# Retention queries: two products of all heads copied out twice with a row mask, instead of four products with half of their columns zero

## What is computed

```
q = jnp.einsum('bhsd,hde->bhse', xh, wq)          # complex
k = jnp.einsum('bhsd,hde->bhse', xh, wk)
v = jnp.einsum('bhsd,hde->bhse', xh, wv)
scores = jnp.einsum('bhse,bhte->bhst', q, k) * _decay_mask(s)
y = jnp.einsum('bhst,bhte->bhse', scores, v).real
mu = y.mean(-1, keepdims=True)
var = y.var(-1, keepdims=True)
yn = (y - mu) * jax.lax.rsqrt(var + 1e-05)
...
out = ((gate * yn).astype(jnp.complex64) @ w2).real
```

## Time and profile before

| | |
|---|---|
| median of 3 runs | 2453.52 us (2449.77 to 2454.09) |
| the profiled execution | 2452.1 us, span of its instructions 2450.3 us |
| busy over the span | PE 87%, PEld 61%, DVE 65%, ACT 50%, POOL 37% |
| chain that ended last | the page's list of its lines has only lines of the last stage |
| retention stage | about 522.8 us to 812.7 us of the span, 290 us |

### The profile page before, as it was taken

The page is one execution under the profiler, slowest core; times in us unless marked ns, Lnnn a source line. Parts: engine busy times, 40 slices in busy tenths (PEclk is TensorE's granted clock), DMA queues, the critical chain, the costliest instruction groups (busy, mean ns, idle before and its releaser), DMA issues. The chain is left out here.

```text
span 2450.3 us, 41718 instructions
## 1 busy us (share of the span) xinstructions
PE 2134.8 (87%) x14183; PEld 1496.8 (61%) x14183; DVE 1588.2 (65%) x3564; ACT 1230.3 (50%) x2063; POOL 915.0 (37%) x763
## 2 busy tenths in 40 slices
PE   5799999979998599999999997999999995776671
PEld 4567868855555466666666664777777774555450
DVE  4432333346777588888888875676767664666673
ACT  2334464344554367677667675555655562332330
POOL 0000000013443378777778772000000001786772
PEclk9999999989999699999999999999999996678995
DMA  7660010019920100000000000000000001214554
GB/s 262 245 245 18 27 34 11 1 43 419 420 117 2 69 1 1 0 0 0 0 0 0 0 1 20 1 0 0 0 0 0 0 1 45 83 43 122 165 154 154
DMA packets 64688, 165.46 MB, mean 68 GB/s; under 512 B 12310, under 2 KB 43460, under 8 KB 55084
## 3 DMA queue, kind: packets, MB, share of 16 engines
q1 hardware_dynamic: 51564, 148.42, 17.0%
q0 software_dynamic: 7104, 12.71, 1.5%
q10 hardware_dynamic: 5888, 2.62, 0.4%
HBM read 68.81 MB, written 96.86 MB: 68 GB/s over the span
## 5 line engine op out<-in xcount | busy, mean ns | idle before, releaser
L1261 POOL TENSOR_TENSOR c_both<-c_hid 128x512 f32<-128x512 f32 x384 | 491.6, 1287 | 144.5 <-ACT c_hid L1234 106.2
L1234 ACT ACTIVATE c_hid<-c_scaled,c_b 128x1024 f32<-128x1024 f32 x384 | 437.1, 1150 | 172.9 <-DVE c_scaled L1308 158.0
L1308 DVE TENSOR_TENSOR c_scaled<-c_p_h,c_shares 128x1024 f32<-128x1024 f32 x384 | 454.5, 1215 | 80.5 <-PE c_p_h L1177 79.5
L1182 PE MATMUL c_p_o<-c_both,c_w 128*128 128x512 f32 x768 | 390.8, 591 | 0.0
L1175 PE MATMUL c_p_h<-c_x_hi,c_w_hi 128*128 128x512 f32 x384 | 291.9, 760 | 2.6 <-DVE c_w_lo L1331 2.6
L624 POOL TENSOR_TENSOR d_ln_rstd<-d_ln_var,d_ln_power 128x2 f32<-128x2 f32 x48 | 33.4, 696 | 525.3 <-DVE d_ln_var L620 525.3
L240 POOL COPY a_work<-a_vec 128x64 f32<-128x64 f32 x4 | 1.2, 303 | 444.4 <-PE a_p_A L322 256.0
L1182 PEld LDWEIGHTS c_p_o<-c_both,c_w 128*128 128x128 f32 x768 | 144.3, 188 | 36.1 <-issue 2.2
L1176 PE MATMUL c_p_h<-c_x_lo,c_w_hi 128*128 128x512 f32 x384 | 152.6, 397 | 0.0
L1492 PEld LDWEIGHTS d_p_s<-d_kk,d_q_bd 128*128 128x128 f32 x768 | 123.9, 192 | 45.9 <-issue 45.9
L1177 PE MATMUL c_p_h<-c_x_hi,c_w_lo 128*128 128x512 f32 x384 | 151.9, 396 | 0.0
(11 more groups left out here) (331 smaller groups left out, 4658.6 us busy)
## 6 DMA issues: line engine op xcount, KB each, us to landing
slots<-b_blank SPq DMA_DIRECT2D x56, 1040.0 KB, 23.7
band_scratch<-a_work SPq DMA_DIRECT2D x16, 1024.0 KB, 5.7
a_work<-band_scratch SPq DMA_DIRECT2D x16, 1023.5 KB, 7.9
e_wb<-e_weights SPq DMA_DIRECT2D x63, 164.0 KB, 2.5
a_raw<-in_Wc SPq DMA_DIRECT2D x16, 512.0 KB, 3.6
e_xb<-slots SPq DMA_DIRECT2D x63, 130.0 KB, 2.2
e_yb<-e_again SPq DMA_DIRECT2D x12, 512.0 KB, 5.6
a_work<-in_x_tok SPq DMA_DIRECT2D x16, 256.0 KB, 8.2
```

Source lines behind the costliest of these rows:

```text
L1182: nc.tensor.matmul(p_o[s][:, 0:N], w2[:, q, :], both[q % SLOTS][:, :], start=(q == 0), stop=(q == NQ - 1)).then_inc(s_down, 1)
L1234: nc.scalar.activation(hid[q % SLOTS][:, :, :], scaled[q % SLOTS][:, :, :], ACT.Gelu, bias=b1[:, q:q + 1]).then_inc(s_ge, 1)
L1261: nc.gpsimd.tensor_tensor(both[q % SLOTS][:, :], hid[q % SLOTS][:, 0, :], hid[q % SLOTS][:, 1, :], ALU.add).then_inc(s_bo, 1)
L1308: v.tensor_tensor(scaled[q % SLOTS][:, :, :], p_h[q % SLOTS][:, 0:N].unsqueeze(1).to_broadcast([128, 2, N]), shares[s][:, :, :], ALU.mult) ...
```

## The change

Queries now come from two products, i = 0 and 1, one for each part, with all columns of the weight in place. ScalarE copies each of the two out twice, with a per-partition scale `half[:, a]` that is one on the rows of head a of every pair and zero on the others. `tq` has the same contents as before. `half` is a new input of 128 x 2 numbers, loaded with the other constants (CONST counts it). NQ falls from 4 to 2 and NP from 6 to 4, so the projections at the end of a body are the values alone. `score_w` is half as large, isn't cleared any more, and is filled by two copies of 128 columns instead of four of 64.

```diff
-        score_w = sb("score_w", [128, 4, 128])
+        score_w = sb("score_w", [128, 2, 128])
+        half = sb("half", [128, 2])
...
-        NQ = 4
+        NQ = 2
         NP = NQ + 2
...
-                             (wv[:, :, :], w["wv"]), (w1[:, :], w["w1"]), (w2[:, :], w["rw2"]), (gn[:, :], w["gn"])):
+                             (wv[:, :, :], w["wv"]), (w1[:, :], w["w1"]), (w2[:, :], w["rw2"]), (gn[:, :], w["gn"]),
+                             (half[:, :], w["half"])):
...
-        CONST = 16 * 6
+        CONST = 16 * 7
...
                     if i < NQ:
-                        nc.scalar.copy(tq[s][:, :, i, :], p_p[i % 2][:, 0:N].rearrange("p (n s) -> p n s", n=GB))\
-                            .then_inc(s_projc, 1)
+                        for a in range(2):
+                            last = nc.scalar.activation(tq[s][:, :, 2 * a + i, :],
+                                                        p_p[i % 2][:, 0:N].rearrange("p (n s) -> p n s", n=GB),
+                                                        ACT.Identity, scale=half[:, a:a + 1])
+                        last.then_inc(s_projc, 1)
                         continue
...
-            act.wait_ge(s_zero, 5)
+            act.wait_ge(s_zero, 4)
+            act.wait_ge(s_const, CONST)
...
-            v.memset(score_w[:, :, :], 0.0).then_inc(s_zero, 1)
...
-            dve.wait_ge(s_zero, 5)
-            for a in range(2):
-                for r in range(2):
-                    heads = "p (j a d) -> p j a d"
-                    last = v.tensor_copy(score_w[:, 2 * a + r, :].rearrange(heads, a=2, d=RD)[:, :, a, :],
-                                         p_p[r][:, 0:128].rearrange(heads, a=2, d=RD)[:, :, a, :])
+            for r in range(2):
+                last = v.tensor_copy(score_w[:, r, :], p_p[r][:, 0:128])
...
+    side = np.arange(128) // RD % 2
+    d["half"] = f(np.stack([side == 0, side == 1], 1).astype(np.float32))
```

## The result

The changed kernel takes 2443.25 us (median of 6 runs, 2441.13 to 2447.97), the kernel before 2453.31 us in the same series (6 runs, 2449.77 to 2454.09). The ratio is 0.9964 with a 95% interval of 0.9951 to 0.9977: faster by 10 us, 0.4%. The forecast was 2444 us, 0.4% faster.

A forecast was written before the change was run, and what follows sets the result against it. TensorE's order and the loop through VectorE and GpSimd's root both take 15.73 us, the second binding after the change. Steady groups 5.5, body 0 1.5 and start 1.6 sum to 8.6 us: forecast 2444 us, range 2438 to 2450.

The forecast's parts named there:

- The bound: Steady groups: TensorE's order and the VectorE-GpSimd root loop both take 15.73 us; once TensorE is faster, the second binds.
- The walk through VectorE's body: VectorE from yn to the variance, TensorE early: pauses before prod and masks 1 close, new interval 15.27 us.
- The term, 12 x 0.46 = 5.5 us: Twelve steady intervals from yn to yn, each 0.46 us shorter: 5.5 us won (2.4 to 7.0).
- The start: Stage start: projections 0.6 us earlier, two products fewer, values falling into the slow-clock stretch: 1.6 us won (1.1 to 3.1).
- Body 0: First body, no yn, TensorE's order sets the pace: the removed pair counts in full, 1.5 us (1.4 to 1.5).
- The last bodies: Last two bodies, without layer norm statistics; masks 2 wait for scores that keep their distance from masks 0: nothing won.
- The sum: Whole kernel: 5.5 + 1.5 + 1.6 = 8.6 us won (4.9 to 11.6).
- The first yn: Sign in the changed kernel's profile: the first yn should start at about 574.4.
- The activation: ScalarE's four scaled query copies: 0.58 us each instead of 479 ns, 0.4 us more per group.
- the wait at the yn columns: TensorE in steady groups of the changed kernel: it should wait some 0.5 us for yn at the yn columns.
- the third rival: ScalarE's queue becomes the bound: threshold 0.7 us per activation, kernel slower from about 0.9; at 1.0, 2457.6 to 2459.0 us; 4%.
- The price of the pair: TensorE, one pair of query products a group: 1.48 us of its time removed.

The follow-up runs named there:

- short_before: Kernel before with GpSimd's root computed for 4 of 32 columns, the rest a constant 1.0: 2448.41 us beside 2454.37, ratio 0.9976.
- short_after: Changed kernel with GpSimd's root computed for 4 of 32 columns, the rest a constant 1.0: 2424.06 us, ratio to the kernel before 0.9879.
- after_again: The changed kernel run once more, nothing altered: ratio to the kernel before 0.9969.
- plain_copies: Changed kernel with the four query copies unscaled, the mask left out: 2445.89 us, ratio to the kernel before 0.9967.
- extra_product: Changed kernel with the first query product computed twice into the same bank: 2446.69 us, ratio to the kernel before 0.9973.
- double_copies: Changed kernel with each scaled query copy done once more into a spare buffer: 2531.68 us beside 2524.31 for the kernel before, ratio 1.0024.
- extra_two: Changed kernel with both query products computed twice into their banks: 2514.30 us beside 2517.58 for the kernel before, ratio 0.9994.

## Why the prediction was right, and where it was off

**The bound (right).** Before, TensorE's loop; after, VectorE's and GpSimd's. short_before and short_after show both halves. One reading was too simple: TensorE does not work "without a break but for 0.73 us". In the kernel before, the fourth scores at 649.47 take 1.26 us instead of 0.90, because they wait for masks 2. It changes nothing in the forecast, since this wait is there with the root cut as well.

**The walk through VectorE's body (right).** Distances from the start of yn, forecast and measured: masks 1 at 2.95 and 2.94, combine at 3.42 and 3.42, statistics at 4.94 and 4.90, masks 2 at 6.92 and 6.88, the variance complete at 9.73 and 9.70. The term, 12 x 0.46 = 5.5 us, came out as 188.78 - 183.28 = 5.50, but from ten intervals of 15.23 or 15.24 (0.49 less than before) and two of 15.43 and 15.51. These two come in the same groups in after_again, plain_copies and extra_product, and in short_after as 14.59 and 14.52. They belong to this program, and I have no cause for them. So the hit of 5.50 against 5.5 is partly luck: each usual interval gave a little more than forecast, and these two gave less.

**The start (right).** From the stage's first DMA to the first masks it was 545.46 - 522.84 = 22.62 us, and is 544.32 - 523.39 = 20.93: 1.69 for the 1.6 forecast. As supposed, the values fell into the slow stretch and took 3.30 us instead of 1.98 (TensorE's timeline, answers to the earlier trace rows):

```profile
534.85 2.93 PE L785 MATMUL b_p_p<-b_xT,b_score_w 128*128 128x384 f32 x4 [0.58 <-DVE b_score_w L1013]
537.73 3.30 PE L791 MATMUL b_p_p<-b_wv,b_xT 128*96 128x256 f32 x8
```

**Body 0 (under-sized).** I had 1.5 us; from the first masks of group 0 to those of group 1 it was 17.52 us and is 15.52, 2.0 less. The removed pair is 1.48 of it. The rest is where the slow clock fell. In the kernel before it took in the gate product, so the second scores and masks 1 came late (masks 1 start 5.36 us behind masks 0), and the third scores waited for masks 1: 1.61 us instead of 0.90 (first fence). In the changed one the gate product still ran fast and combine was slow, masks 1 came 4.33 us behind masks 0, and the third scores did not wait (second):

```profile
547.78 1.54 PE L795 MATMUL b_p_p<-b_xT,b_w 128*128 128x384 f32 x2
549.25 1.55 PE L755 MATMUL b_p_s<-b_tq,b_xT 32*96 32x384 f32 x8
550.73 0.87 PE L765 MATMUL b_p_y<-b_sm,b_val 96*32 96x96 f32 x32
...
552.10 1.61 PE L755 MATMUL b_p_s<-b_tq,b_xT 32*96 32x384 f32 x8
```

```profile
546.37 0.84 PE L797 MATMUL b_p_p<-b_xT,b_w 128*128 128x384 f32 x2
547.14 1.51 PE L757 MATMUL b_p_s<-b_tq,b_xT 32*96 32x384 f32 x8
548.58 1.51 PE L767 MATMUL b_p_y<-b_sm,b_val 96*32 96x96 f32 x32
...
550.91 0.90 PE L757 MATMUL b_p_s<-b_tq,b_xT 32*96 32x384 f32 x8
```

**The last bodies.** Forecast nothing, measured 0.1 us. The sum, forecast as 8.6 us, is 9.3 us in the stage.

**What was luck.** The median of 2443.25 us lies within 1 us of the forecast of 2444, but executions of one kernel differ by 4 to 7 us, and the other stages took 3.4 us of the profiled execution's gain back. The first yn at 574.36, forecast as 574.4, is a coincidence too: the stage started 0.55 us later and won 0.6 us more on the way there than forecast.

**ScalarE.** The activation took 581 ns for 580. The queue had more room than I gave it: some 0.6 us around the values' copies, and 0.99 us between the loops instead of the 0.5 of the wait at the yn columns. The step that was off is that I took a visible wait for the whole slack. It left the forecast untouched, but it set the third rival's threshold too near.

**The price of the pair.** 1.48 us is right for what the loop lost (short_before and short_after), but putting the pair back costs only 1.30 to 1.32 of it.

## What to carry to other kernels

An engine at 95% may share its bound with a loop of other engines that closes in the same time: before pricing work taken from it, look for the in-order engine with a long wait at a fixed place in its body, and count how much of the rest of its body is pause. That sum is about what the change can win per round; here it was 0.4 us, and 0.5 was won, out of 1.48. And the slack of an engine is better read as the difference of the two loops' lengths, which one run with the other loop cut shows, than as the one wait that the timeline prints: part of it can stand inside rows that merely look longer.

## What the runs showed that I had not expected

- The half clock came in the middle of a steady stage in double_copies, after TensorE had stood 0.56 and 1.32 us within 6 us: 3.5 us at 0.52, and an interval of 17.56 us instead of 15.5. It came behind one group only, though three earlier ones have the same waits. With waits of 0.73 and 0.49 us a group, in the changed kernel, the granted clock stayed at 1.00 through all steady groups.
- The 96x32 root on GpSimd takes 5.42 us and the 96x4 root 1.00, so 28 columns cost 4.4 us. In this stage that root, on an engine busy 43% of the time, is what the whole loop hangs on.
- Among others like it, a 128x384 float32 product costs TensorE 0.65 us from start to start (extra_two); a pair by itself takes 1.48 us up to the values.
